# Self attention with another step order: where row sums and value projections stand among the score blocks

## The reference

```python
qkv = X @ W_qkv                                   # X is the layer-normed x
qkv = qkv.reshape(b, s, h, d, 3)                  # s = 512, h = 16, d = 64
q, k, v = (qkv[..., 0], qkv[..., 1], qkv[..., 2])
scores = jnp.einsum('bqhd,bkhd->bhqk', q, k) / scale
weights = jax.nn.softmax(scores, axis=-1)
attn = jnp.einsum('bhqk,bkhd->bqhd', weights, v)
return attn.reshape(b, s, h * d) @ W_out
```

## Time and profile before

| | us |
|---|---|
| median of three runs | 3017.0 (3009.43 to 3017.76) |
| profiled execution, span from first to last instruction | 3008.1 |
| PE busy | 2752.6 (92%) |
| DVE busy | 1923.9 (64%) |
| ACT busy | 1450.5 (48%) |
| POOL busy | 1104.9 (37%) |

### The profile page before, as it was taken

One profiled execution on the slowest core, in us unless ns is written; L12 is line 12 of the kernel. 1 busy time (PEld: TensorE's weight loads), 2 busy tenths in 40 slices (PEclk: granted clock), 3 DMA queues, 4 the chain that ended last, 5 costly groups with the idle time before them and its releaser, 6 DMA issues. The chain is left out here.

```text
span 3008.1 us, 49289 instructions
## 1 busy us (share of the span) xinstructions
PE 2752.6 (92%) x16604; PEld 1616.4 (54%) x16605; DVE 1923.9 (64%) x3109; ACT 1450.5 (48%) x2231; POOL 1104.9 (37%) x853
## 2 busy tenths in 40 slices
PE   7997899999868899999999999999889999966998
PEld 4774333333335555555555555555445555556997
DVE  5775776667668766757575757575645555474565
ACT  3342566666668643434343434343335555553333
POOL 3233332222037243434343434443443333153333
PEclk9998899999989999999999999999989999958999
DMA  5002222222111000000000000000043222146665
GB/s 159 0 0 74 54 57 57 55 59 53 34 56 43 1 1 1 0 0 0 0 0 0 0 0 0 0 0 0 1 112 78 72 67 70 45 114 233 216 218 193
DMA packets 102929, 159.71 MB, mean 53 GB/s; under 512 B 28350, under 2 KB 63433, under 8 KB 97161
## 3 DMA queue, kind: packets, MB, share of 16 engines
q1 hardware_dynamic: 97784, 147.88, 17.1%
q0 software_dynamic: 3408, 8.46, 0.8%
q10 hardware_dynamic: 1600, 1.61, 0.2%
HBM read 91.79 MB, written 14.96 MB: 35 GB/s over the span
## 5 line engine op out<-in xcount | busy, mean ns | idle before, releaser
L1672 DVE TENSOR_REDUCE self_nmax<-self_SM 128x2 f32<-128x1024 f32 x256 | 313.9, 1226 | 184.5 <-PE self_SM L1569 177.7
L522 DVE TENSOR_REDUCE cross_nmax<-cross_S 128x2 f32<-128x1024 f32 x256 | 311.9, 1224 | 150.5 <-PE cross_S L347 149.6
L1650 ACT ACTIVATE self_PT<-self_ST 128x1024 f32<-128x1024 f32 x256 | 262.6, 1026 | 292.0 <-PE self_ST L1592 292.0
L1710 POOL TENSOR_TENSOR self_U<-self_PT 128x1024 f32<-128x1024 f32 x64 | 153.0, 2391 | 622.1 <-ACT self_PT L1650 622.1
L1713 POOL TENSOR_TENSOR self_U<-self_U,self_PT 128x1024 f32<-128x1024 f32 x128 | 304.0, 2375 | 55.6 <-ACT self_PT L1650 51.1
L456 ACT ACTIVATE cross_PT<-cross_S 128x1024 f32<-128x1024 f32 x256 | 260.9, 1026 | 114.6 <-PE cross_S L358 113.9
L1186 DVE TENSOR_REDUCE cross_nmax<-cross_S 128x4 f32<-128x1024 f32 x128 | 156.8, 1225 | 143.4 <-PE cross_S L984 143.3
L1602 PE MATMUL self_OP<-self_PT,self_V 128*64 128x512 f32 x1024 | 233.8, 598 | 10.1 <-ACT self_PT L1650 10.1
L1686 DVE RECIPROCAL self_rcp<-self_W 128x512 f32<-128x512 f32 x64 | 214.1, 3345 | 8.4 <-PE self_W L1609 8.4
L1112 ACT ACTIVATE cross_PT<-cross_S 128x1024 f32<-128x1024 f32 x128 | 131.1, 1024 | 119.6 <-PE cross_S L1000 119.6
L1602 PEld LDWEIGHTS self_OP<-self_PT,self_V 128*64 128x64 f32 x1024 | 69.5, 136 | 139.2 <-issue 132.8
(11 more groups left out here) (436 smaller groups left out, 6335.7 us busy)
## 6 DMA issues: line engine op xcount, KB each, us to landing
moe_staged<-in_L_ffn_W SPq DMA_DIRECT2D x36, 1024.0 KB
cross_ks<-cross_parts SPq DMA_DIRECT2D x384, 64.0 KB, 2.2
cross_qs<-cross_parts SPq DMA_DIRECT2D x376, 64.0 KB, 2.3
all_x<-in_L_ffn_W SPq DMA_DIRECT2D x14, 1024.0 KB
all_x<-sorted_rows SPq DMA_DIRECT2D x83, 130.0 KB, 2.3
cross_cT<-in_ctx_T SPq DMA_DIRECT2D x16, 512.0 KB, 4.5
sorted_rows<-all_spare_row SPq DMA_DIRECT2D x1, 5460.0 KB, 23.8
all_x<-in_x SPq DMA_DIRECT2D x8, 512.0 KB, 3.7
```

Of the source, the lines that this page charges most:

```text
L522: dve.tensor_reduce(nmax[:, g % 2, 0:R, n % PER_G], S[:, slot[st], :, :], AX.X, ALU.max, negate=True).then_inc(s_maxed, 1)
L1650: act.activation(PT[:, k, :, :], ST[:, :, :], ACT.Exp).then_inc(exped.sem, 1)
L1672: dve.tensor_reduce(nmax[:, i, 0:P:D], SM[:, :, :], AX.X, ALU.max, negate=True).then_inc(maxed.sem, 1)
L1710: pool.tensor_tensor(U[:, c % 2, :, :], PT[:, 0, :, :], PT[:, 1, :, :], ALU.add).then_inc(added.sem, 1)
```

## The change

It only changes the order of steps in `plan`. Three things move within a chunk:

- the `sum` of the chunk before goes from the third block (k = 2) to the end of the fourth (k = 3), behind `mt` and right ahead of `av`;
- the value projection goes from the fourth block into the third; in chunks 6 and 7, where there are two, the second goes from behind `av` into the fourth block, ahead of `mt`;
- in the last chunk, its own `sum` comes right behind `av` and ahead of the next `max`.

In chunk 5 `norm` keeps its blocks, but its second half comes ahead of `mt`. The same reordering shows in the opening pass, whose list is cut from the same loops: its steps are then q0, k0, v0, v1, max0, max1, q1, max2, k1, max3, v2, v3, mt0, max4; before it was q0, k0, v0, max0, v1, max1, q1, max2, k1, max3, mt0, v2, max4, v3.

```diff
@@ -1415,24 +1415,24 @@
                         add("stat", 1, 1)
                     if c == 3:
                         add("htok", 1, 1)
-                    if c == 5:
-                        add("norm", KC, KC)
-                    if c:
-                        add("sum", c - 1, NC)
-                else:
-                    add("mt", c + 1, NC)
                     if c < NT:
                         add("v", NT + c, HALF * NT)
                     if c == 5:
+                        add("norm", KC, KC)
+                    if c >= 6:
+                        add("v", HALF * NT + 2 * (c - 6), HALF * NT)
+                else:
+                    if c == 5:
                         add("norm", KC + 1, KC)
                     if c >= 6:
-                        add("v", HALF * NT + 2 * (c - 6), HALF * NT)
+                        add("v", HALF * NT + 2 * (c - 6) + 1, HALF * NT)
+                    add("mt", c + 1, NC)
+                    if c:
+                        add("sum", c - 1, NC)
             add("av", c, NC)
-            add("max", (c + 2) * NT, NC * NT)
             if c == NC - 1:
                 add("sum", c, NC)
-            if c >= 6:
-                add("v", HALF * NT + 2 * (c - 6) + 1, HALF * NT)
+            add("max", (c + 2) * NT, NC * NT)
         for i in range(NT):
             add("out", i, NT)
         return steps
```

## The result

The changed kernel takes 3032.5 us (median of 5 runs, 3030.5 to 3036.2), the kernel before 3013.1 us (5 runs, 3009.4 to 3017.8): a ratio of 1.0062 with a 95% interval of 1.0052 to 1.0073, so 19.4 us slower. The spans of the profiled executions are 3008.1 and 3030.0, 21.9 apart. The forecast was 3047 with a range of 3029 to 3056: slower as said, by two thirds of the forecast loss.

The account below looks back on a forecast made before the run. TensorE, 97% busy in self attention, was taken to set the time. Seven loop batches at 4.2 us (29.2), last batch +2.0 and opening pass -1 gave +30 us on 3017, so 3047 us, range 3029 to 3056.

Parts of the forecast that it names:

- The exchange of fillers: Third and fourth blocks: value projection and row sums swap places, costing an ordinary chunk 0.0 to 0.2 us on TensorE alone.
- The multiply at 0.69: VectorE's multiply by the reciprocals (L1689) takes 0.69 us instead of 1.80, as GpSimd's last sum is over.
- the heavy rival: VectorE's multiply stays at 1.80 us, six chunks of each batch pay 1.11 more, 3099 us; chance 0.04.
- The ordinary chunk: Late reciprocal and multiply delay the next reduction; TensorE's next row-maximum product comes at 11.30 instead of 10.91, +0.39 us.
- 4.2 us per batch: Sum of the eight chunks' added times in a self-attention loop batch, 29.2 us over seven batches.
- Seventh chunk: The projection no longer hides the next batch's first row-maximum reduction; query projection at 13.31 instead of 12.48, +0.83 us.
- Eighth chunk: No projection covers the last reciprocal; the output product's eighth term comes at 16.37 instead of 15.05, +1.33 us.
- The low end, 3.2: Loss per loop batch in us by the low ends of the chunk terms, 22.5 us over seven batches.
- the light rival: VectorE's multiply ends in time, ordinary chunks cost nothing; 2.0 us per batch, +14 in all, 3031 us; chance 0.11.
- The signs: Self attention: multiplies near 0.69 us, L1569 waits from 0.8 to near 1.1, batch 147.7, last-multiply wait about 1 us.
- Opening pass and last batch: Self attention outside the loop: opening pass -1 us (between -2 and 0), last batch +2.0 us (1.2).
- The clock rival: Last stage, 2642 to 2734: granted clock rises from 0.50 to 2.4 GHz, up to 23 us back, 3016 us; chance 0.05.

Follow-up runs that it names:

- x3_both: Changed kernel with the multiply behind the next reduction and the second projections of chunks seven and eight put back behind the weighted values: 3015.35 us against 3015.38, ratio 1.0001.
- x1_late: Changed kernel with only VectorE's multiply moved behind the next chunk's first reduction, except in a batch's last chunk: 3024.6 us, batch 145.00.
- x4_proj_alone: Changed kernel with the row sums put back in the third block, behind the projection, so only the value projections move: 3044.9 us, batch 147.74.
- x7_fast: Kernel before, reordered: query and key projections between score block and row-maximum product, row sums, reciprocal, multiply and value projection moved too: 2999.4 us against 3015.4, ratio 0.9949.
- x8_first: The faster reordering of the kernel before, with VectorE's row-maximum reduction ahead of the query or key projection's low part: 2985.5 us against 3015.4, ratio 0.9900.

## Why the prediction was right, and where it was too large

- **TensorE's queue sets the time, and VectorE's rest is what is spent.** Right. TensorE's idle time grew by 15.1 us in six batches, 10.2 of it before the row-maximum products.
- **The exchange of fillers costs an ordinary chunk 0.0 to 0.2 us on TensorE alone.** Right: x3_both keeps it, and its second, third, fifth and sixth chunks are within .04 of the kernel before. Fourth block 2.96 behind the third (forecast 2.95), transposes 4.09 (4.09), row sums 4.68 (4.68), weighted values 5.59 (5.69).
- **The multiply at 0.69.** Right, in all 64; the heavy rival is refuted. The trace agrees with the rule quoted there from the Trainium skill (SBUF — State Buffer, Who interferes with whom): with GpSimd's addition over, the same multiply takes 0.69 in place of 1.80.
- **The ordinary chunk.** Mechanism right, as x1_late shows. Multiply at 9.39 (forecast 9.41), reduction 10.00 (10.05), next product 11.27 (11.30).
- **The term that was mis-sized is "4.2 us per batch",** above all by its step that the reciprocal starts 1.26 after the row sums. In the earlier trace rows it starts at 1502.34 because VectorE's own reduction has just ended there, as this row of the kernel before shows:

```profile
1501.19 1.23 DVE L1672 TENSOR_REDUCE self_nmax<-self_SM 128x2 f32<-128x1024 f32 x1
```

So that number was not the time from the row sums to a reciprocal that is waiting for them. In the changed kernel VectorE is waiting, and the distance is 1.22 in the second chunk, 1.13 in the third, fourth, fifth and seventh and 1.07 for the last row sums. That is about half of the 1.4 us by which the batch was over-priced (an estimate, the sum of these differences from 1.26). A like error, a distance taken from a row with other neighbours, stands in the seventh and eighth chunk for projection plus transposes: the changed kernel's seventh chunk takes 2.01 from the projection to the row sums, where the forecast has 4.09 to 6.26, 2.17. TensorE there, and the reciprocal, before which VectorE had waited 4.53 us:

```profile
1592.85 0.49 PE L1536 MATMUL self_W<-self_wv,self_hT_hi 128*128 128x512 f32 x1
...
1594.34 0.60 PE L1576 MATMUL self_W<-all_ident,self_nmax 128*128 128x128 f32 x4
1594.86 1.08 PE L1609 MATMUL self_W<-self_U,self_ones 128*64 128x512 f32 x4
```
```profile
1595.99 3.36 DVE L1686 RECIPROCAL self_rcp<-self_W 128x512 f32<-128x512 f32 x1 [4.53 <-PE self_W L1609]
```

- **Seventh chunk.** Row sums 6.10 (forecast 6.26), reciprocal 7.23 (7.52), query projection 13.02 (13.31): +0.55 for +0.83.
- **Eighth chunk.** The last row sums at 10.45 (forecast 10.85), with the earlier ones 0.91 and the weighted values 3.43 long in place of 1.01 and 3.58; the reciprocal 1.07 behind them for 1.26; so the eighth term at 15.75 for 16.37. By the table the chunk holds 0.5 of the 1.4 us.
- **The low end, 3.2, was too high as well.** It varied one spacing (0.41 or 0.59), which turned out to be 0.59, and none of the lengths that were wrong. The measured 2.75 lies between it and the light rival's 2.0 per batch.
- **The time fell inside the range partly by its margins.** The loss of 19.4 us is below the forecast's own 22 to 31. 3032.5 is inside 3029 to 3056 because the low end was taken down for the light rival and for the spread of the kernel before. Of the 14.5 us between 3047 and 3032.5, 10.6 are the loss and 3.9 the base, 3017.0 where the median is now 3013.1.
- **The light rival.** In time it came nearer (3031), but its mechanism is refuted: it had ordinary chunks cost nothing, and the reduction starts at 10.00, not at 9.64, at a cost of 0.35 us in the second chunk. Its sum left that cost out and put 0.4 too much on the eighth chunk.
- **The signs.** The batch is 146.29 for 147.7. The loader's wait for the row maxima before L1569 went from a mean of 0.8 us (29.7 in 36) to 1.0 (42.6 in 42), and TensorE's new wait for the last multiply is 0.6 for about 1.
- **Opening pass and last batch.** Forecast -1 and +2.0; in the second profiles, without a clock fall, -0.9 and +1.1. The bare first reduction costs 1.33 (forecast 1.4). With 19.2 for the loop the sum is 19.4.
- **The clock rival.** Refuted: 0.52 in the late stage.

## What to carry to other kernels

An engine's rest in front of an operation that another engine waits for is not free: ask whether that operation will still start the moment its input is there. The distance from one engine's row to the row on another that needs its result can be carried over only if the second engine stood idle before it started; otherwise it measures the work that it was busy with. Where one order holds several hole fillers, price the whole exchange, put work with no waiter behind what the busiest engine waits for, and keep a projection between a product whose result is reduced and the next use of that result.

## What the runs showed of the hardware

- Four row-sum products directly ahead of the weighted values take 0.91 us from start to start and the sixteen behind them 3.53; apart (x4_proj_alone, the kernel before) 1.01 to 1.03 and 3.58. Why neighbours save 0.15 was not tried by itself.
- VectorE's multiply of 128x512 with two SBUF inputs takes 0.68 to 0.70 us alone and, beside GpSimd's addition, 1.4 to 2.3 in the kernel before; in x7_fast and x8_first some take 0.75 to 1.0, and the longest 2.6. The 45.5 us that VectorE works less in six batches did not make the kernel faster. The short multiply still kept the loss small: it stands in TensorE's way now, as x1_late shows.
- The granted clock falls to about 0.5 for 3.4 to 6.8 us in some executions and not in others of the same program; ahead of the one shown TensorE was busy 2.2 of 4.0 us. Pass and batch were 1.5 and 2.1 us longer with a fall than without, and the start of self attention differs by up to 9 us between profiles (1027.6 to 1036.8): single spans can't settle a difference of that size, durations of a batch can.
